# One list of rows per expert over all batches, three tables of whole blocks, and new places for tiles and routing steps

## What is computed

```python
probs = softmax(flat @ gate_W)
topk_w, topk_idx = top_k(probs, 2); topk_w /= topk_w.sum(-1)
out = 0.5 * gelu(flat @ shared_W + shared_b)
for e in range(8):
    h = gelu(flat @ W1[e] + b1[e])
    out += combine[:, e] * (h @ W2[e] + b2[e])
out = layernorm(out) * gamma + beta        # then gated and added to x
```

## Time and profile before

| | |
|---|---|
| median of 3 runs | 1118.73 us (1104.53 to 1119.12) |
| span of the profiled execution | 1110.3 us (its time outside the span is not shown) |
| PE busy | 929.3 us (84%) |
| DVE busy | 759.5 us (68%) |
| ACT busy | 589.6 us (53%) |
| POOL busy | 460.1 us (41%) |
| tile transposes on PE | 78, the first at 867.4 us, the last at 1074.1 us |

### The profile page before, as it was taken

The page is one execution under the profiler, slowest core; times in us unless marked ns, Lnnn a source line. Parts: engine busy times, 40 slices in busy tenths (PEclk is TensorE's granted clock), DMA queues, the critical chain, the costliest instruction groups (busy, mean ns, idle before and its releaser), DMA issues. The chain is left out here.

```text
span 1110.3 us, 23738 instructions
## 1 busy us (share of the span) xinstructions
PE 929.3 (84%) x7248; PEld 596.8 (54%) x7248; DVE 759.5 (68%) x1948; ACT 589.6 (53%) x1257; POOL 460.1 (41%) x632
## 2 busy tenths in 40 slices
PE   5389898989798998997299899899898789987982
PEld 3023232323232333332298787788788779886761
DVE  2578797878688788889478856655656566663552
ACT  1048677777577676776034435525533475754551
POOL 5121222323231304130424446755752545765772
PEclk9999899999899899999589999999998899998996
DMA  4523232323150515170161001001100112223332
GB/s 134 134 102 88 103 97 98 102 92 108 39 153 14 166 35 168 36 240 12 47 237 58 16 16 34 28 24 30 31 18 18 47 38 61 70 62 106 107 93 76
DMA packets 56332, 87.09 MB, mean 78 GB/s; under 512 B 10388, under 2 KB 41186, under 8 KB 55568
## 3 DMA queue, kind: packets, MB, share of 16 engines
q1 hardware_dynamic: 45392, 53.75, 17.2%
q0 software_dynamic: 10816, 31.84, 8.0%
HBM read 45.83 MB, written 40.24 MB: 78 GB/s over the span
## 5 line engine op out<-in xcount | busy, mean ns | idle before, releaser
L680 DVE TENSOR_REDUCE nmax<-ps_s 128x1 f32<-128x512 f32 x512 | 321.8, 683 | 68.8 <-PE ps_s L861 67.1
L574 ACT ACTIVATE p_ring<-ps_t 128x512 f32<-128x512 f32 x512 | 286.8, 598 | 133.0 <-PE ps_t L872 130.1
L861 PE MATMUL ps_s<-k_stack,q_stack 56*128 56x512 bf16 x512 | 184.6, 409 | 35.2 <-DMA q_stack<-q_parts_dram 16.0
L872 PE MATMUL ps_t<-q_stack,k_stack 59*128 59x512 bf16 x512 | 188.0, 396 | 5.7 <-ACT p_ring L574 2.6
L885 PE MATMUL ps_av<-p_ring,v_ext 128*32 128x256 f32 x2048 | 168.1, 401 | 3.4 <-ACT att L584 2.3
L861 PEld LDWEIGHTS ps_s<-k_stack,q_stack 56*128 56x128 bf16 x512 | 39.9, 94 | 167.8 <-DVE nmax L680 92.0
L1408 POOL DMA_INDIRECT back_dram<-weights,target x78 | 88.3, 1132 | 73.6 <-DVE weights L2018 49.8
L1674 ACT ACTIVATE weights<-a,wtile 128x128 f32<-128x128 f32 x312 | 89.5, 374 | 36.5 <-PE a L2281 35.7
L2292 PE MATMUL a<-wtile,weights 128*128 128x128 f32 x624 | 86.1, 282 | 17.1 <-DVE weights L2018 9.8
L1581 ACT ACTIVATE hid<-a 128x512 f32<-128x512 f32 x64 | 38.2, 598 | 110.0 <-PE a L2103 109.7
L1422 POOL DMA_INDIRECT rows_dram<-hrow,slot x64 | 65.8, 1028 | 74.0 <-DVE y L1772 43.9
(11 more groups left out here) (277 smaller groups left out, 1500.6 us busy)
## 6 DMA issues: line engine op xcount, KB each, us to landing
rows_dram<-wmod POOLq DMA_DIRECT2D x8, 2340.0 KB, 8.5
k_stack<-k_parts_dram SPq DMA_DIRECT2D x32, 192.0 KB
q_stack<-q_parts_dram SPq DMA_DIRECT2D x32, 192.0 KB
xt<-rows_dram SPq DMA_DIRECT2D x78, 65.0 KB, 1.9
wall<-in_wall SPq DMA_DIRECT2D x1, 4112.0 KB, 13.4
q_parts_dram<-q_parts SPq DMA_DIRECT2D x32, 128.0 KB, 2.4
weights<-back_dram SPq DMA_DIRECT2D x8, 512.0 KB, 4.2
k_parts_dram<-k_parts SPq DMA_DIRECT2D x24, 128.0 KB, 2.3
```

The lines of the kernel that those rows point to most:

```text
L574: nc.scalar.activation(probs[:, u % RING, :], ps_t[u % TBANKS][:], ACT.Exp, scale=HD ** -0.5).then_inc(exp_done, 1)
L680: nc.vector.tensor_reduce(nmax[:, js, n:n + 1], ps_s[u % SBANKS][:], AX.X, ALU.max, negate=True).then_inc(max_done, 1)
L861: nc.tensor.matmul(ps_s[u % SBANKS][:], q_stack[par][row:row + STACK, c, quarter(t)], k_stack[par][row:row + STACK, c, :], start=True, sto ...
L872: nc.tensor.matmul(ps_t[u % TBANKS][:], k_stack[par][rows_, c, quarter(t)], q_stack[par][rows_, c, :], start=True, stop=True).then_inc(t_f ...
```

## The change

There is one list per expert over all eight batches, so only one padding per expert: (8192 + 8 x 127) // 128 = 71 tiles. Three tables name the tiles in turn. The first names those blocks of 128 rows that are surely full after the batches 0 to 5 (41 of them), the second the further ones that are surely full after batch 6 (8), the third the remaining 22, among them the last, partly filled blocks. Since a table names at least as many full blocks as it has tiles, what it leaves over is carried to the next table as an "old" segment; each table works over 16 segments, 8 old and 8 new. Tables are made in the stages 5, 6 and 7. The routing steps' places are given per stage (`ROUTE_PLACES`; `None` is for stages 0 to 4), as are those of the row sends and of the tiles: 22 in stage 6, 27 in stage 7, 22 behind. Sums stand after the tiles 60, 61, 63, 66, 69 and 70 (before: 59, 62, 65, 68, 71 and 74 of 78).

```diff
+def sure_blocks(n):
+    return -(-(2 * T * n - E * (P - 1)) // P)
+PART_TILES = (sure_blocks(FIRST), sure_blocks(B - 1) - sure_blocks(FIRST),
+              (2 * T * B + E * (P - 1)) // P - sure_blocks(B - 1))
+OLD_TILES = PART_START[2] + E
...
+ROUTE_PLACES = {
+    None: {
+           "norm2_T": 7, "logits": 9, "comb_T": 20, "ranks": 22, "biases": 23, "counts": 29, "save_hTf": 8,
+           "exp_router": 10, "gelu_shared": 17, "save_combT": 23, "shift_logits": 11, "shared": 12, "best_two": 13, "combine": 19,
+           "fill_rows": 20, "find_slots": 23, "start_base": 24, "table": 30},
+    5: {
+           "norm2_T": 2, "logits": 4, "comb_T": 11, "ranks": 12, "biases": 14, "counts": 16, "save_hTf": 2,
+           "exp_router": 7, "gelu_shared": 10, "save_combT": 11, "shift_logits": 3, "shared": 4, "best_two": 8, "combine": 9,
+           "fill_rows": 10, "find_slots": 13, "start_base": 14, "table": 18},
+    6: {
+           "norm2_T": 6, "logits": 8, "comb_T": 16, "ranks": 17, "biases": 18, "counts": 20, "save_hTf": 5,
+           "exp_router": 11, "gelu_shared": 12, "save_combT": 20, "shift_logits": 7, "shared": 8, "best_two": 11, "combine": 15,
+           "fill_rows": 18, "find_slots": 19, "start_base": 20, "table": 25},
+    7: {
+           "norm2_T": 2, "logits": 7, "comb_T": 11, "ranks": 13, "biases": 14, "counts": 22, "save_hTf": 5,
+           "exp_router": 8, "gelu_shared": 11, "save_combT": 12, "shift_logits": 6, "shared": 7, "best_two": 9, "combine": 10,
+           "fill_rows": 11, "find_slots": 13, "start_base": 20, "table": 22},
+}
+ROW_PLACES = {5: (15, 16, 22, 28),
+            6: (21, 22, 24, 25),
+            7: (17, 18, 19, 21)}
+TILES_IN = {6: (0, 0, 0, 0, 0, 0, 1, 0, 1, 1, 1, 1, 2, 1, 0, 2, 0, 0, 0, 0, 1, 0, 0, 3, 0, 0, 1, 2, 2, 1, 2, 0),
+            7: (2, 1, 2, 1, 0, 0, 0, 2, 0, 1, 3, 1, 2, 0, 0, 0, 0, 0, 1, 2, 0, 2, 1, 0, 0, 2, 0, 0, 0, 1, 1, 2)}
+SUM_AFTER = (60, 61, 63, 66, 69, 70)
...
-        SOONER = {5: 4, 6: 5, 7: 6, 8: 7, 11: 8, 12: 9, 13: 10, 15: 11, 16: 11, 18: 12, 19: 13, 20: 13, 21: 14,
-                  24: 15, 26: 16}
...
             sp.wait_ge(table_ready, 1)
-            for j in range(PART_TILES[0]):
+            for j in range(PART_START[1]):
                 load_rows(j)
...
             gate_rows(gate_end[:], 5, 2, gate_end_in)
+            sp.wait_ge(sent[FIRST % 2], SENDS * (FIRST // 2 + 1))
+            sp.wait_ge(table_ready, 2)
+            for j in range(PART_START[1], PART_START[2]):
+                load_rows(j)
...
-            sp.wait_ge(table_ready, 2)
-            for j in range(PART_TILES[0], TILES):
+            sp.wait_ge(table_ready, 3)
+            backs = 0
+            for j in range(PART_START[2], TILES):
                 load_rows(j)
-                if j == PART_TILES[0] + XT:
+                if j == OLD_TILES + XT:
...
+                    for m in range(3):
+                        load_back(m)
...
-            for m in range(first_stored, FIRST - 2):
+            for m in range(2):
                 store(m)
...
-            for m in range(max(first_stored, FIRST - 2), B):
+            for m in range(2, B):
                 store(m)
...
+                        for n, q in enumerate(ROW_PLACES[b]):
+                            work[q].append(lambda q=q: pace(q // 4 - (q % 4 < 2)))
+                            own_sends(q, 2 * n, 2 * n + 1)
...
+                table(nc.vector.tensor_copy(count_s[:], c1[:, 0:E]))
+                if n == 0:
+                    whole_blocks_into(seg_n[:, 0, old])
+                elif n == 1:
+                    whole_blocks_into(seg_n[:, 1, new])
+                    table(nc.vector.tensor_tensor(seg_n[:, 1, new], seg_n[:, 1, new], seg_n[:, 0, old], ALU.subtract))
...
+                table(nc.vector.tensor_tensor_scan(until[:, 1:2 * E + 1], one_row[:], seg_n[:, n, :], 0.0, ALU.mult,
+                                                   ALU.add))
...
+                assert done[0] == TABLE_DONE[n + 1]
```

214 lines of the change are left out of this document (126 added, 88 removed).

## The result

The changed kernel takes 1073.61 us (median of 4 runs, 1073.2 to 1077.09); the kernel before, run beside it, 1111.63 us (4 runs, 1102.4 to 1119.12). The ratio is 0.9694, 95% interval [0.9649, 0.9739]: faster by 3.1%. The forecast was 1090.8 us, range 1073 to 1106, so the time lies 0.6 us inside the lower edge of the range: 27.9 us were forecast and 38.0 us were won. The profiled execution of the changed kernel has a span of 1075.4 us and a time of 1077.09 us, 1.7 us more.

A forecast was written before the change was run, and what follows sets the result against it. TensorE nearly bounds loop stages (plus short waits) and bounds tile stretches; tile start, list change and end are not TensorE-bound. Terms -13.2 - 4 + 0 - 3 + 3 - 6.4 - 2.6 - 2.2 + 0.5 = -27.9: 1118.7 to 1090.8 us, range 1073 to 1106.

The forecast's parts named there:

- Against which time: Sum made on the profiled span of 1110.3 us; the 8.4 us up to the median of 1118.7 carried over unchanged.
- Seven tiles, -13.2: Tile stretches: 78 to 71 tiles, each 1.89 us of TensorE, -13.2 us.
- Start, -4: Start of the tiles: they begin some 3.5 us earlier and `norm2_T` falls into the wait, -4 us.
- Stage 5, 0: Stage 5 itself: longer table, about 4.5 us, against routing steps done earlier; 0, bounds -3 and +4 us.
- Loop places, -3: Stages 0 to 4: new routing places shorten waits ahead of `values` and `att_T`, -3 us.
- Tiles among the steps, +3: Stages 6 and 7: 49 tiles at 32 places, one table more, +3 us over the waits of before.
- From list to list, -6.4: Change of tile lists: 9.4 us of waits and slow first tile go, 3 us kept for sends' landing, -6.4 us.
- Sums and end: End: sixth sum behind the last tile -2.6, last tile's send sooner -2.2, more stores +0.5 us.
- More falls away: Rival, chance 0.18: `values` waits no more, stages 6, 7 and list change cost nothing extra; -12 more, about 1078 us.
- The waits refill: Rival, chance 0.17: saved waits come back in stages 6 and 7, only the stretch behind pays; -15.6, about 1103 us.
- The gate load: Rival, chance 0.04: the gate load's landing delay stands bare in the middle of stage 7; +4.8, 1096 us.
- The clock falls in the gaps: Rival, chance 0.05: clock falls at the 13 runs of places without a tile in stages 6 and 7; about 1145 us.

## Why the prediction was nearly right, point by point

*The whole.* The time is 17.2 us under the forecast: 7.1 because the median before came out at 1111.6 us and not 1118.7, and 10.1 because the change gave 38.0 us and not 27.9. The parts missed on both sides (5.0 too little in the loop stages, 5.8 too little in the tiles, 5.7 too much at stage 5 and the start, by the table). That the range holds the time, by 0.6 us, is in part luck.

*What bounds it.* Right: the tiles' stretch gave most, -26.7 us, and 20.9 were forecast for it. What the sum lacked there is by the rows the clock, which no edit was made to show. From the first W1 product to the first sum, 5 to 8% of the clock were not granted before and 2 to 3% as changed; that is an estimate of 8 to 13 and 2 to 4 us of these 149 to 162, by the price of a spell in the loop stages (1.5 to 1.8 us for 0.04 of 40 us). Only 1.36 us of it, the slow first tile of the second list, was in the sum.

*Against which time.* Wrong. Of the 8.4 us carried from the span to the median, 6.7 were the difference between executions: from span to time it is 1.6 to 1.7 us in the second execution of the kernel before and in both of the changed one. The sum on the spans, 1082.4 forecast and 1075.4 and 1068.5 measured, has to be judged without them: -27.9 against -38.6 on the mean of two traces each.

*Seven tiles, -13.2.* Right in the direct price (12.9 to 13.7 in the trace with seven more). The company of 3 us, a longer wait for ACT with slow clock behind it, was not in the sum.

*Start, -4.* Too large. From the start of the last `scatter` to the first W1 product it fell from 9.33 to 7.70 us; with the 0.6 us of `norm2_T` inside, -2.2. The first tile's transpose, forecast 3.5 us sooner, came 6.3 us behind that start and not 7.5, 1.2 sooner. `shift_2` ended 5.4 us behind that start (8.5 before) and not 4.1, and then `norm2_T` and two tile transposes came, at the slow clock, ahead of the product: what I had put into the wait stands behind it.

*Stage 5, 0.* Mis-sized, towards its upper bound. At a clock of 1.00 it takes 41.39 us from `attend` to `attend`, and 37.30 in the kernel before with the new loop places: +4.1, nearly a bare table of 4.76 us. Then -1.3 up to the last `scatter` (8.80 for 10.06): +2.8. So the two steps together lost 0.6 us (1.2 by the stretch at equal clock, less the 0.6 of `norm2_T`) where I had -4.

*Loop places, -3.* The mechanism was right and its size nearly, -4.7 at equal clock: `values` and `att_T` wait less, `combine` is off the chain, and `logits` cost nothing, because `norm1_T` waits where it stood. What the sum lacked was that the clock changes the length of each stage by up to 3.5 us, in one way or the other; in ten executions this gave 3.3 us more.

*Tiles among the steps, +3.* Mis-sized, near 0. The waits among the steps are 10.7 us, and 11.4 before; behind the second table's 4.26 us TensorE waits 1.33 us, and not 3. With the old places the kernel is slower, by 6.6 us in the medians and 2.4 to 2.8 in the traces. I had counted a table more and the waits of before besides; the runs of places without a tile stand where those waits would hold it.

*From list to list, -6.4.* Nearly right: 0.49 + 2.32 + 1.34 = 4.2 us of waits are left of 9.4 (5.0 in the second trace), where I kept 3. The 2.32 us, though, are the third table, which I had not put on this path; for a send's landing, which I had, 1.34 us are left.

*Sums and end.* The sum of the three terms: right. From the last tile's W2 product to the end it is 31.5 to 32.1 us in three executions before and 30.1 to 30.7 in eight as changed, -1.5 where 2.2 less 0.5 were forecast, and the sixth sum now lies inside this stretch, under the wait for the back load. The send alone: it went 1.95 us behind its rows and not 0.8 (3.0 before), because `bias_end(4)`, 1.27 us on POOL, stands ahead of it.

*The rivals.* "More falls away" forecast 1078, and came nearest. Of its terms, `values` waiting no more did not come (5.7 us are left), and in stages 6 and 7 and between the lists waits are left too; the clock, which it did not name, gave more. "The waits refill" is refuted by the time and by the waits up to the first sum, 15.6 us for 19.4. The gate load, loaded from 956.22 us on, can have cost no more than the 0.49 us for which a tile waited for its rows at 963.45 us (its chance also stood in the wrong place: 1090.8 + 4.8 = 1095.6 is under 1096.4). "The clock falls in the gaps" is refuted as to tiles, 0.95 to 1.00 granted from 856 to 994 us; its price of 1.9 us was 1.7 by its own rows, since 4 us at 0.60 and 0.55 do the work of 2.3. By the Trainium skill, "TensorE: Matmul & The Clock Gate", section "HAM oscillation — how this bites in real kernels", a kernel whose bursts of matmuls are parted by waits for DMAs pays for the slow clock anew at each burst; the waits of its example are longer than those in the rival's gaps. Here the trace agrees behind the waits of 1.99 us at 928.45 and 2.44 us at 1031.47, with one slow spell each, and does not behind the 2.32 us at 974.65, where 954 to 986 us were granted 1.00; and the wait of 2.44 us had no spell behind it in three other executions.

*The signs.* The tables took 4.76, 4.26 and 3.1 us (4.5, 4.5 and 3 forecast), and no wait between tile 40 and tile 50 is over 3 us. The loop stages, 37.4 to 41.1 us, lie on both sides of the 39 to 40 forecast, and one is over the 41 that was to show the forecast wrong: that is the clock, 1.00 to 0.92.

## What to carry to other kernels

Split a span at events that both programs have and write down each part's granted clock: a difference between two executions can be larger than the effect of the edit, and only stages at equal clock show it. Empty places in an order are worth keeping where a step waits for another engine, since work put there is held behind it. A chain of small serial instructions on VectorE can be paid wherever it stands: moving the first table (4.76 us) within stage 5 moved the wait, and did not take it away. What such a chain costs is the wait of the busy engine behind it, 1.33 us for the second table and 2.32 of 3.1 for the third.

## What of the hardware had not been expected

The same instructions of the same program ran at another clock in another execution: the six stages of the changed kernel had 4 spells of low clock in one and 1 in the other, each costing 1.5 to 1.8 us. And even the part ahead of them, where no line was changed, took from 601.1 to 613.7 us. By the Trainium skill, "TensorE: Matmul & The Clock Gate", section "What's actually happening", the number of matmuls at the slow clock at a kernel's start differs from run to run of one kernel, and the loss there is under 1% of a typical span. In these traces it is not the start alone that differs: the five stages in the middle took from 190.2 to 200.5 us with the same steps, 0.9% of the span by themselves. Where a spell begins was found (behind one wait, that of `values`), but not what decides whether it does: the same wait of 1.05 us was followed by one in some stages and not in others. It does not look like chance from stage to stage either: four executions, with edits behind these stages or none, had the same clocks stage by stage, and lengths of these five stages from 193.98 to 194.10 us.
